# The first pass and the last stage of a Mamba-2, attention and expert decoder on one core: transposes inside a unit, five moved steps, contexts drawn ahead, ones columns beside the values

## The chip, the cores and the metric

The kernel is one program on one core of a Trainium2 chip. TensorE (PE in the rows) multiplies and transposes, VectorE (DVE) and ScalarE (ACT) read and write SBUF and PSUM, GpSimd (POOL) works on SBUF only, SyncE (SP) issues the DMAs. The metric is the device time of one execution in microseconds. Less is better.

## The reference, cut to what matters

Three residual layers run over 32 sequences of 64 tokens with 512 features, 2048 tokens in all. Most of the work is the first layer.

```python
x = x + mamba2(layernorm(x))              # 128 heads of 64, 8 groups, state 128
x = x + attention(layernorm(x), ctx)      # 32 query heads, 8 key heads of 16, per sequence
x = x + experts(layernorm(x))             # 4 low-rank experts (rank 16), top 2

proj = h @ in_proj_w.T                    # gate 8192, xBC 10240, dt 128
xBC = silu(conv4(xBC) + conv_b)           # depthwise, 4 taps
y = ssd(xs, A, B, C, D, softplus(dt))     # decayed scores per head, times x
g = y * silu(gate)
g = g * rsqrt(mean over each group's 1024 (g*g) + eps) * norm_w
return g @ out_w.T

scores = q k / 4 + mask;  probs = softmax(scores);  out = probs @ ctx
```

Keys and values of the attention are both the rows of `ctx` (64 by 128 for each sequence).

## The kernel before, in words

**The main loop.** Tokens are taken in four blocks of 512 (`tb`), and in each block the eight groups (`g`) follow one another: 32 iterations, `n = 8 tb + g`. An iteration has 18 *units* (`unit(k, ...)`), each 12 matmuls of 128x512 that project the block on 128 rows of `in_proj_w`. Unit 0 gives B, unit 1 C, and then even units give x for channel tile c, odd units the gate for it. Units alternate between the two PSUM banks `p_in[0]` and `p_in[1]`. An even unit's bank is read by ScalarE (`tap0`) and VectorE (`conv`), then `silu` makes `x_t`; `to_tokens(c)` transposes `x_t` on TensorE into `p_in[1]`; `x_tokens(c)` (VectorE) scales it into `x_tok`; `heads(c)` multiplies two channel tiles at a time with `decay` into `p_y`; `skipped` and `gated` (VectorE) make `t_y` and `g_f`. ScalarE and GpSimd split `g_f` in `g_hi` and `g_lo`, and `project(c)` multiplies both with `o_ring` into the four banks `p_out`, 12 matmuls, three for each 128 tokens.

`decay` is made in a chain for each block of 8 heads: GpSimd subtracts (`differences`), VectorE clamps (`clamped`), ScalarE takes the exponential (`exp`), VectorE multiplies by the scores (`decayed`). `exp` needs another function table than `silu`: each change is an ACT_TABLE_LOAD.

**The first pass** is the first iteration (n = 0, "not begun"). It has its own order, with `decay` of block 0 in two halves. All along it also splits the raw weights: ScalarE writes the high part, GpSimd (`w_low`, line 1722) and VectorE (`refill_o`, line 1258) the low part. `normal(QT, ...)` is the layernorm of the next block's first tile, which `normal_tile` transposes.

**The end.** Attention and experts of a tile of 128 tokens are spread over the main loop for 12 of the 16 tiles. The last four tiles (`q` = 0 to 3) can only start once the last group's output is summed. After the loop come: the last `heads`, `project(5)`, `experts_in` of loop tile 11, `project(6)`, `mean_squares` (the sum of squares over the group, as products of `ss` with a column of ones), `project(7)` tile by tile (`part_done`), and meanwhile the root mean square (`variance` on VectorE, `inverse_rms` on GpSimd). `accumulate_tile(q)` (VectorE, line 1667) is then the first step of each of the four tiles.

**The tables.** The four tiles' steps (k = 0 to 16) and the last three steps of loop tile 11 (17 to 19) are put in order by `waves`: for each engine a table of places, sorted. An engine does its steps in that order and in no other. The steps are: 0 accumulate, 1 context (transposed, copied, and made into `kbd` and `v2` by GpSimd), 2 query rows, 3 and 5 scores of each half, 4 and 6 maxima, shift and exponential, 7 and 8 transposed probabilities, 9 values, 10 and 11 divide and add, 12 expert rows, 13 low rank, 14 logits, 15 experts, 16 delta and result. Each tile has two PSUM banks `y0`, `y1`.

The softmax totals of these four tiles come out of TensorE: beside each 32 columns of values, a product of the same probabilities with two columns of `v2m` gives two totals.

The contexts of the four tiles are loaded by SyncE after the last `heads` (`load_context`: three DMAs for a tile, one of `ctx`, two of `v2r`), in the order q = 0, 1, 2, 3.

Of the kernel before, what the change touches and what calls it, by code (L numbers as in the profile page):

```python
# [38 lines left out]
def decoder_kernel(nc, x, ctxv, amask, wt, wdt, owt, params, dtb, alog, ffa, ffb,  # L39
# [10 lines left out]
    with outer:  # L50
# [72 lines left out]

        TILE_WIDE = (("sc", [2, 2, 2 * KV // 2, SEQ]), ("row", [HID]), ("col", [KT, P]), ("x2s", [HID]))
        TILE_REST = (("p_t", [REP, KV // 2, P]), ("ctx", [P]), ("ctx_t", [P]), ("v2r", [2, P]), ("v2", [2, P]), ("kbd", [2, KV // 2, SEQ]),
# [55 lines left out]
        v2_done = sem("v2_done"); kbd_done = sem("kbd_done"); part_done = sem("part_done"); sum_done = sem("sum_done")  # L181
# [50 lines left out]
        TAIL_PE = (56, (1452, 584, 672, 741, 1521, 826, 942, 895, 922, 959, 298, 1336, 1458, 1515, 1693, 1691, 1764, 1085, 0, 650))  # L232
        TAIL_ACT = (73, (851, 454, 558, 1395, 841, 215, 887, 854, 918, 2146, 1536, 514, 1382, 1475, 1572, 1741, 1676, 0, 106, 1977))
        TAIL_DVE = (97, (242, 0, 355, 575, 664, 746, 748, 691, 89, 2397, 972, 1001, 1094, 512, 1344, 1479, 1932, 347, 371, 492))
        TAIL_POOL = (105, (856, 981, 857, 1965, 1662, 1957, 1729, 2327, 670, 1771, 1993, 2018, 1301, 2835, 1361, 1816, 1018, 0, 232, 1822))

        def waves(stage, places):

            step, stages = places
            turns = [(at + step * q, q, k) for q in range(QT) for k, at in enumerate(stages) if q == 0 or k < 17]  # L240
            for _, q, k in sorted(turns):
                y0, y1 = ((p_in[0][:, :], p_in[1][:, :]), (p_y[:, 0, :], p_y[:, 1, :]),
                          (p_out[0][:, :], p_out[1][:, :]), (p_out[2][:, :], p_out[3][:, :]))[q]
                stage(k, q, LOOP_TILES + q, tail_tiles[q], y0, y1)
# [28 lines left out]
        def _(sp):  # L273
# [193 lines left out]
        def _(pe):  # L467
# [38 lines left out]
            def unit(k, tb, g, n):  # L506
# [24 lines left out]
                for w, a in ((0, 0), (0, 1), (1, 0)):  # L531
                    for kt in range(KT):
# [133 lines left out]
            def values(t, S, y0, totals=None):  # L666
# [3 lines left out]
                for r in range(REP):  # L670
                    for gp in range(KV // 2):
                        for s in range(2):
                            rows = slice(s * SEQ, (s + 1) * SEQ)
                            ins = mm(y0[rows, r * P + gp * 32:r * P + gp * 32 + 32], S.p_t[:, r, gp, rows],
                                     S.v2[:, s, gp * 32:(gp + 1) * 32], True, True)
                            if totals is not None:
# [508 lines left out]
        def _(dve):  # L1185
# [466 lines left out]
            for c in range(2):  # L1652
                dve.wait_ge(sq_done, CPG * ITERS - 1 + c)
                ins = V.tensor_tensor(ss[:, :], ss[:, :], g_sq[:, c, :], ALU.add)
                if c == 0:
                    link(ins)
# [279 lines left out]
```

## Time and profile before

| | us |
|---|---|
| median of 3 runs | 2863.83 |
| the 3 runs | 2863.83, 2866.99, 2861.97 |
| the profiled execution, its own time | 2870.87 |
| its span, first to last instruction | 2869.1 |

The profiled execution took 1.77 us more than its span, and is 7.0 us above the median of the runs. TensorE is busy 2828.2 us of the span (99%), VectorE 1999.2, ScalarE 1453.9, GpSimd 1316.5. From 200 to 2700 us TensorE has hardly a gap; the two stages that the change touches are the first 100 us and the last 85 us.

The profile's rows give for a group of instructions: start, length, engine, line, operation, tile written <- tiles read, shape, count, and in brackets the idle time just before with what ended it.

### The profile page before, as it was taken

The numbers are of one execution on the slowest core, as the hardware profiler recorded it, in microseconds if no ns is written. First come the engines' busy times: TensorE is split into PE (matmuls) and PEld (weight loads), VectorE is DVE, ScalarE is ACT, GpSimd is POOL, SyncE is SP. The second block draws the span as 40 slices with busy tenths as digits, with TensorE's granted clock in tenths as the row PEclk, the third lists the DMA queues.
The fourth block names the chain that finished last, engine by engine and source line by source line (L and its number), as shares of the span: only waits on it lengthen the run. The fifth ranks groups of instructions, "written<-read, shape, count | busy, mean of one in ns | idle before, by whom it ended". The sixth has DMA issues, their size and how long they took to land.

```text
span 2869.1 us, 56835 instructions
## 1 busy us (share of the span) xinstructions
PE 2828.2 (99%) x22480; PEld 2288.3 (80%) x22480; DVE 1999.2 (70%) x3154; ACT 1453.9 (51%) x2185; POOL 1316.5 (46%) x832
## 2 busy tenths in 40 slices
PE   7999999999999999999999999999999999999998
PEld 5788888778788788887888888888887888878876
DVE  7777768887667667677666666677666576666667
ACT  5666566655445535445445454544445354454443
POOL 4767767775344333443342443433444334433423
PEclk9999999999999999999999999999999999999997
DMA  7788777878566555555565564565665555555630
GB/s 242 266 303 290 264 269 258 274 254 289 182 196 194 177 184 184 184 184 187 194 198 185 187 198 162 187 194 171 200 199 181 185 188 186 185 190 170 197 105 20
DMA packets 179431, 578.30 MB, mean 202 GB/s; under 512 B 25249, under 2 KB 31905, under 8 KB 171105
## 3 DMA queue, kind: packets, MB, share of 16 engines
q1 hardware_dynamic: 179168, 574.66, 60.9%
q8 instruction: 182, 2.98, 0.4%
q14 instruction: 81, 0.66, 0.1%
HBM read 460.29 MB, written 114.29 MB: 200 GB/s over the span
## 4 chain that ended last, share of the span: by engine, by line
PE 92%; DVE 5%; ACT 1%; issue 1%; POOL 0%; DMA 0%; DVEq 0%; SPq 0%; ACTq 0%; POOLq 0%
PE p_in L469 53%; PE p_out L469 24%; PE p_y L469 9%; PE p_in L557 4%; DVE cv L1318 1%; PE p_y L663 1%; DVE o_ring L1258 1%; DVE t_y L1367 1%; DVE g_f L1379 1%; ACT cv L861 0%; DVE cum L1280 0%; DVE decay L1350 0%; PE p_y L685 0%; PE p_y L634 0%; DVE cum L1272 0%
## 5 line engine op out<-in xcount | busy, mean ns | idle before, releaser
L469 PE MATMUL p_in<-xnb,w_ring 128*128 128x512 f32 x6864 | 1683.4, 398 | 0.9 <-DVE cv L1318 0.9
L469 PEld LDWEIGHTS p_in<-xnb,w_ring 128*128 128x128 f32 x6864 | 1263.7, 189 | 266.5 <-issue 1.6
L1318 DVE SCALAR_TENSOR_TENSOR cv<-p_in,cpar,cv 128x504 f32<-128x504 f32 x954 | 700.0, 734 | 469.3 <-ACT cv L861 445.8
L1730 POOL TENSOR_TENSOR g_lo<-g_f,g_hi 128x512 fp32r<-128x512 f32 x256 | 342.5, 1339 | 1202.5 <-ACT g_hi L861 1202.5
L469 PE MATMUL p_out<-o_ring,g_hi 128*128 128x512 f32 x2048 | 639.0, 393 | 1.1 <-POOL g_lo L1730 1.1
L861 ACT ACTIVATE cv<-p_in,cpar 128x512 f32<-128x512 f32 x318 | 246.4, 775 | 642.0 <-PE p_in L469 604.4
L469 PEld LDWEIGHTS p_out<-o_ring,g_hi 128*128 128x128 f32 x2048 | 379.6, 188 | 81.8 <-issue 1.3
L469 PE MATMUL p_out<-o_ring,g_lo 128*128 128x512 f32 x1024 | 400.0, 391 | 0.0
L1355 DVE TENSOR_TENSOR x_tok<-p_in,dts 128x512 f32<-128x512 f32 x256 | 176.5, 690 | 290.0 <-PE p_in L557 288.5
L861 ACT ACTIVATE x_t<-cv 128x512 f32<-128x512 f32 x256 | 160.9, 628 | 309.3 <-DVE t_y L1367 285.9
L1741 POOL TENSOR_TENSOR ss<-ss,g_sq 128x512 f32<-128x512 f32 x190 | 309.3, 1628 | 7.5
L1784 POOL TENSOR_TENSOR decay<-decay,cumk 128x2048 f32<-128x2048 f32 x63 | 234.6, 3724 | 33.6 <-DMA decay<-cum_scr 33.6
L861 ACT ACT_TABLE_LOAD x183 | 234.8, 1283 | 4.0 <-PEq L1930 0.7
L1722 POOL TENSOR_TENSOR w_ring<-raw_w,w_ring 128x512 fp32r<-128x512 f32 x144 | 208.5, 1472 | 59.5 <-ACT w_ring L861 43.9
L861 ACT ACTIVATE sg<-p_in 128x512 f32<-128x512 f32 x254 | 149.0, 587 | 167.4 <-PE p_in L469 167.4
L469 PEld LDWEIGHTS p_out<-o_ring,g_lo 128*128 128x128 f32 x1024 | 192.2, 188 | 41.2
L1367 DVE SCALAR_TENSOR_TENSOR t_y<-x_t,dpar,p_y 128x256 f32<-128x256 f32 x512 | 210.9, 475 | 0.9 <-PE p_y L469 0.9
L1379 DVE TENSOR_TENSOR g_f<-t_y,sg 128x512 f32<-128x512 f32 x256 | 182.6, 754 | 0.0
L861 ACT ACTIVATE g_hi<-g_f 128x512 fp32r<-128x512 f32 x256 | 159.3, 623 | 34.4 <-DVE g_f L1379 33.9
L469 PEld LDWEIGHTS p_y<-decay,x_tok 64*64 64x64 f32 x8192 | 131.6, 135 | 49.3 <-issue 49.3
L557 PE MATMUL p_in<-id_sb,x_t 128*128 128x128 f32 x1024 | 158.0, 277 | 7.4 <-ACT sg L861 5.0
L557 PEld LDWEIGHTS p_in<-id_sb,x_t 128*128 128x128 f32 x1024 | 118.2, 141 | 50.7 <-issue 21.2
(259 smaller groups left out, 2298.9 us busy)
## 6 DMA issues: line engine op xcount, KB each, us to landing
w_ring<-ws_scr SPq DMA_DIRECT2D x432, 512.0 KB, 3.7
o_ring<-ows_scr SPq DMA_DIRECT2D x192, 512.0 KB, 4.6
ws_scr<-w_ring SPq DMA_DIRECT2D x144, 512.0 KB, 5.7
decay<-cum_scr SPq DMA_DIRECT2D x126, 512.0 KB, 6.8
raw_w<-wt SPq DMA_DIRECT2D x144, 256.0 KB, 5.0
ows_scr<-o_ring SPq DMA_DIRECT2D x64, 512.0 KB, 6.0
raw_o<-owt SPq DMA_DIRECT2D x64, 256.5 KB, 5.3
acb<-x SPq DMA_DIRECT2D x3, 1024.0 KB, 7.2
```

Source lines behind the costliest of these rows:

```text
L469: return nc.tensor.matmul(o, lhsT=l, rhs=r, start=first, stop=last)
L557: ins = nc.tensor.transpose(p_in[1][:, q * P:(q + 1) * P], x_t[:, c % 2, q * P:(q + 1) * P], id_sb[:, :])
L663: ins = nc.tensor.transpose(banks[rl][:, gp * P:(gp + 1) * P], pv, id_sb[:, :])
L861: return nc.scalar.activation(dst, src, func, **kw)
L1318: ins = V.scalar_tensor_tensor(acc[:, :, t:SEQ], src[:, :, 0:SEQ - t], cpar[:, 5 * m + 3 - t:5 * m + 4 - t], acc[:, :, t:SEQ], ALU.mult, A ...
L1355: V.tensor_tensor(x_tok[:, c % 2, :, :].rearrange("p q (h d) -> p q h d", h=2), p_in[1][:, :].rearrange("p (q h d) -> p q h d", q=QT, h=2) ...
L1367: ins = V.scalar_tensor_tensor(t_y[:, c % 2, :].rearrange(by_seq, q=QT, s=2)[:, s], x_t[:, c % 2, :].rearrange(by_seq, q=QT, s=2)[:, s], d ...
L1379: V.tensor_tensor(g_f[:, c % 2, :], t_y[:, c % 2, :], sg[:, (CPG * n + c) % GATES, :], ALU.mult).then_inc(g_done, 1)
L1722: T(w_ring[:, k % RING_W, 1, :, :].rearrange("p k c -> p (k c)"), raw_w[:, (UNITS * g + k) % RAW_W, :], w_ring[:, k % RING_W, 0, :, :].rea ...
L1730: T(g_lo[:, c % 2, :], g_f[:, c % 2, :], g_hi[:, c % 2, :].bitcast(F32), ALU.subtract).then_inc(glo_done, 1)
L1741: T(ss[:, :], a, g_sq[:, c % 2, :], ALU.add).then_inc(ss_done, 1)
L1784: T(decay[:, blk, :, :, :], decay[:, blk, :, :, :], last.unsqueeze(3).broadcast_to([P, 8, QT, SEQ]), ALU.subtract) \
```

## The change

What it does, by place:

- **First pass.** `to_tokens(1)` moves into unit 6, behind its first 4 matmuls (argument `between`). Unit 8 moves ahead of `to_tokens(2)`. `normal(QT, ...)` moves ahead of `conv(5)`. `clamped(1)` and the refill of `o_ring` 2 and 3 move from step 3 to step 4; `exp(1)` moves from step 3 to step 4 and `decayed(1)` from step 4 to step 5, and so does one load of the silu table.
- **Last iteration.** `to_tokens(7)` moves between the two halves of `project(4)`.
- **Behind the loop.** The contexts of q = 0, 1, 2 are transposed ahead of `project(6)`, all into `p_in[0]`, and copied by ScalarE in one stretch; the fourth becomes step 20 of the tables. VectorE's two additions of `g_sq` to `ss` are gone, and TensorE multiplies both `g_sq` halves with the ones as well (12 products of one column for 4), between the halves of `project(6)`. `skipped` and `gated`, `g_high` and `square` go channel by channel.
- **Ones columns.** `v2` gets 34 columns for each pair of heads, the last two filled by ScalarE (`ones_out`) with the columns of `v2m`, so one product of 34 columns replaces the two of 32 and 2. The reciprocal reads the two banks in two instructions.
- **Tables and banks.** New places for all four engines, written out for each tile, and tiles 1 to 3 in other banks. Step 17 is now the low rank part of loop tile 11.
- **SyncE** issues the same DMAs in the same order; the wait ahead of the fourth context is on `ms_done` in place of `ss_done`.

```diff
-        TAIL_PE = (56, (1452, 584, 672, 741, 1521, 826, 942, 895, ...
+        TAIL_PE = {2: (2, 4, 10, 13), 3: (3, 5, 12, 14), 5: (6, 9, 16, 20), ...
...
+        TAIL_BANKS = ((p_in[0][:, :], p_in[1][:, :]), (p_out[0][:, :], p_out[1][:, :]),
+                      (p_out[2][:, :], p_out[3][:, :]), (p_y[:, 0, :], p_y[:, 1, :]))
...
             for q in range(QT):
                 if q == 3:
-                    sp.wait_ge(ss_done, SUMS * ITERS)
+                    sp.wait_ge(ms_done, ITERS)
...
                 for w, a in ((0, 0), (0, 1), (1, 0)):
+                    if a == 1 and between is not None:
+                        to_tokens(between, n)
                     for kt in range(KT):
...
+            def values_totals(q, t, S, banks):
...
+                for r in range(REP):
+                    for gp in range(KV // 2):
+                        at = (r % 2 * (KV // 2) + gp) * VW
+                        for s in range(2):
+                            rows = slice(s * SEQ, (s + 1) * SEQ)
+                            ins = mm(banks[r // 2][rows, at:at + VW], S.p_t[:, r, gp, rows], S.v2[:, s, gp, :], True, True)
...
-                    unit(6, tb, g, n)
-                    to_tokens(1, n)
+                    unit(6, tb, g, n, 1)
...
+                    if k == 2 and not begun:
+                        unit(8, tb, g, n)
+                    if final(n) and k == CPG - 1:
+                        project(k - 3, tb, n, range(0, 2))
...
             experts_in(LOOP_TILES - 1, loop_tile, y0)
-
-            project(CPG - 2, NTB - 1, ITERS - 1)
-            mean_squares(ITERS - 1)
+            for q in range(QT - 1):
+                pe.wait_ge(tail_in[q], 48)
+                context_in(LOOP_TILES + q, tail_tiles[q], p_in[0][:, q * P:(q + 1) * P])
+
+            project(CPG - 2, NTB - 1, ITERS - 1, range(0, 2))
+            pe.wait_ge(ss_done, SUMS * ITERS - 2)
+            pe.wait_ge(sq_done, CPG * ITERS)
+            pe.sem_inc(hold, 1)
+            for h in range(QT):
+                tok = slice(h * P, (h + 1) * P)
+                mm(p_y[:, 1, h:h + 1], ss[:, tok], ones[:, :], True, False)
+                mm(p_y[:, 1, h:h + 1], g_sq[:, 0, tok], ones[:, :], False, False)
+                ins = mm(p_y[:, 1, h:h + 1], g_sq[:, 1, tok], ones[:, :], False, True)
+            ins.then_inc(ms_done, 1)
+            project(CPG - 2, NTB - 1, ITERS - 1, range(2, QT))
...
-                    if k == (2 if begun else 3):
+                    if k == (2 if begun else 4):
                         exp(1, n)
...
+            for c in (CPG - 2, CPG - 1):
+                g_high(c, ITERS - 1)
+                square(c, ITERS - 1)
+            act.wait_ge(ct_done, LOOP_TILES + QT - 1)
+            for q in range(QT - 1):
+                context_out(LOOP_TILES + q, tail_tiles[q], p_in[0][:, q * P:(q + 1) * P])
...
+                    if k == 3 and not begun:
+                        normal(QT, xt[:, :], xt[:, :], QT)
                     conv(2 + k, n)
...
-                    if k == (3 if begun else 4):
+                    if k == (3 if begun else 5):
                         decayed(1, n)
```

TensorE in the first pass, from the scores of B and C (`c_t,b_t`) to the first output product, before (`p_in<-id_sb,x_t` is a `to_tokens`, `p_y<-decay,x_tok` a `heads`):

```order
L469 MATMUL p_y<-c_t,b_t 64x64 x8
L557 MATMUL p_in<-id_sb,x_t 128x128 x4
L469 MATMUL p_in<-xnb,w_ring 128x512 x12
L557 MATMUL p_in<-id_sb,x_t 128x128 x4
L469 MATMUL p_y<-decay,x_tok 64x64 x32
L469 MATMUL p_in<-xnb,w_ring 128x512 x12
L557 MATMUL p_in<-id_sb,x_t 128x128 x4
L469 MATMUL p_in<-xnb,w_ring 128x512 x24
L469 MATMUL p_out<-o_ring,g_hi 128x512 x2
```

The same place of the changed kernel:

```order
L471 MATMUL p_y<-c_t,b_t 64x64 x8
L561 MATMUL p_in<-id_sb,x_t 128x128 x4
L471 MATMUL p_in<-xnb,w_ring 128x512 x4
L561 MATMUL p_in<-id_sb,x_t 128x128 x4
L471 MATMUL p_in<-xnb,w_ring 128x512 x8
L471 MATMUL p_y<-decay,x_tok 64x64 x32
L471 MATMUL p_in<-xnb,w_ring 128x512 x24
L561 MATMUL p_in<-id_sb,x_t 128x128 x4
L471 MATMUL p_in<-xnb,w_ring 128x512 x12
L471 MATMUL p_out<-o_ring,g_hi 128x512 x2
```

The second transposes stand 8 matmuls earlier, the third 12 matmuls later.

ScalarE in the first pass, from the splits of step 3 to the conv tap of step 5, before (`cv` is `tap0`, `sg` the gate, `decay` the exponential of block 1):

```order
L861 ACTIVATE w_ring<-raw_w 128x512 x4
L861 ACT_TABLE_LOAD
L861 ACTIVATE decay<-decay 128x2048
L861 ACTIVATE cv<-p_in,cpar 128x512
L861 ACT_TABLE_LOAD
L861 ACTIVATE spare<-half_neg 128x1
L861 ACTIVATE x_t<-cv 128x512
L861 ACTIVATE sg<-p_in 128x512
L861 ACTIVATE g_hi<-g_f 128x512
```

The same place of the changed kernel:

```order
L896 ACTIVATE w_ring<-raw_w 128x512 x4
L896 ACTIVATE cv<-p_in,cpar 128x512
L896 ACTIVATE x_t<-cv 128x512
L896 ACTIVATE sg<-p_in 128x512
L896 ACTIVATE g_hi<-g_f 128x512
```

The exponential and two table loads no longer stand ahead of the taps and the silu of step 4; they follow one step later.

TensorE behind the loop, before, from the rows of loop tile 11 (`row_l`) through `project(6)` to the products with ones and the first of `project(7)`:

```order
L685 MATMUL p_y<-id_sb,row_l 128x128 x4
L469 MATMUL p_out<-o_ring,g_hi 128x512 x2
L469 MATMUL p_out<-o_ring,g_lo 128x512
...
L469 MATMUL p_y<-ones,ss 128x1 x4
L469 MATMUL p_out<-o_ring,g_hi 128x512 x2
L469 MATMUL p_out<-o_ring,g_lo 128x512
```

The same place of the changed kernel (six matmuls of `project(6)` stand where the first gap is, six more behind the ones):

```order
L699 MATMUL p_y<-id_sb,row_l 128x128 x4
L632 MATMUL p_in<-id_sb,ctx 128x128 x3
L471 MATMUL p_out<-o_ring,g_hi 128x512 x2
L471 MATMUL p_out<-o_ring,g_lo 128x512
...
L471 MATMUL p_y<-ones,ss 128x1
L471 MATMUL p_y<-ones,g_sq 128x1 x2
```

Three transposes of contexts stand ahead of `project(6)`, each behind its tile's DMAs, and the products with ones have moved from behind `project(6)` into its middle and are three times as many.

## Rows read from the trace of the kernel before

**Rows 1.** Windows: stretch, length, busy PE, PEld, DVE, ACT, POOL, granted clock, DMA

```profile
200.00:2700.00 2500.00, 2495.57 (x19632) 2022.05 (x19634) 1733.22 (x2704) 1265.56 (x1888) 1131.55 (x703) 1.00 0.62 204
2795.59:2866.62 71.03, 62.24 (x802) 46.62 (x800) 56.60 (x144) 26.41 (x52) 26.98 (x24) 0.78 0.05 17
```

**Rows 2.** Timeline of PE, the first pass

```profile
49.92 0.60 PE L557 MATMUL p_in<-id_sb,x_t 128*128 128x128 f32 x4
52.52 1.65 PE L469 MATMUL p_y<-decay,x_tok 64*64 64x64 f32 x64 [2.01 <-DVE decay L1337]
...
82.28 0.63 PE L557 MATMUL p_in<-id_sb,x_t 128*128 128x128 f32 x4 [2.59 <-ACT sg L861]
82.66 7.35 PE L469 MATMUL p_in<-xnb,w_ring 128*128 128x512 f32 x24
...
102.94 5.76 PE L469 MATMUL p_in<-xnb,w_ring 128*128 128x512 f32 x24
```

**Rows 3.** Timelines of DVE, ACT and POOL, the first pass

```profile
50.55 0.69 DVE L1355 TENSOR_TENSOR x_tok<-p_in,dts 128x512 f32<-128x512 f32 x1 [3.15 <-PE p_in L557]
51.16 1.22 DVE L1337 TENSOR_TENSOR decay<-decay,cbt 128x1024 f32<-128x1024 f32 x1
...
56.03 4.29 DVE L1379 TENSOR_TENSOR g_f<-t_y,sg 128x512 f32<-128x512 f32 x2
...
74.98 1.92 ACT L861 ACTIVATE decay<-decay 128x2048 f32<-128x2048 f32 x1
...
55.48 3.70 POOL L1784 TENSOR_TENSOR decay<-decay,cumk 128x2048 f32<-128x2048 f32 x1
...
63.03 3.15 POOL L1730 TENSOR_TENSOR g_lo<-g_f,g_hi 128x512 fp32r<-128x512 f32 x2
```

**Rows 4.** SyncE's timeline behind the last heads; landing times of the v2r DMAs

```profile
2786.02 0.33 SPq L340 DMA_DIRECT2D ctx<-ctxv  x1
...
2790.56 1.25 SPq L342 DMA_DIRECT2D v2r<-ctxv  x2
...
DMA to landing us min/median/max: 2.2/2.3/3.4
```

**Rows 5.** Timeline of PE behind the loop

```profile
2784.81 1.16 PE L469 MATMUL p_y<-decay,x_tok 64*64 64x64 f32 x64 [0.83 <-issue]
...
2793.26 0.95 PE L469 MATMUL p_y<-ones,ss 128*128 128x1 f32 x8
...
2801.80 0.42 PE L698 MATMUL p_y<-id_sb,midg_l 128*64 128x128 f32 x1 [3.83 <-DVE midg_l L1543]
```

**Rows 6.** Windows of PE: length, busy, granted clock, DMA

```profile
2800.00:2801.00 1.00, 0.00 (x0) 0.85 0.00 0
...
2807.00:2808.00 1.00, 1.00 (x16) 0.74 0.04 10
...
2843.00:2869.00 26.00, 22.35 (x116) 0.50 0.11 41
```

**Rows 7.** Timelines of POOL and DVE in the last stage

```profile
2794.48 1.01 POOL L1745 TENSOR_TENSOR rms<-msv,half_neg 128x4 f32<-128x4 f32 x1 [2.93 <-DVE msv L1383]
...
2795.59 0.75 DVE L1667 SCALAR_TENSOR_TENSOR acb<-p_out,rms,acb 128x512 f32<-128x512 f32 x1 [1.18 <-POOL rms L1745]
...
2846.00 0.36 DVE L1684 RECIPROCAL rs<-p_out 128x32 f32<-128x32 f32 x1 [4.41 <-PE p_out L469]
```

**Rows 8.** The chain that ended last, with PE's timeline of the loop tile's values

```profile
2770.00 2.72 PE p_out L469 x12
...
2772.65 2.06 PE L469 MATMUL p_y<-v_l,p_t_l 128*64 128x32 f32 x64
...
2821.06 3.85 PE p_in L469 x128
```

**Rows 9.** PE's timeline, the product with wb at either clock

```profile
2741.07 1.12 PE L469 MATMUL p_y<-wb,m_t_l 64*128 64x512 f32 x2
...
2857.41 2.07 PE L469 MATMUL p_in<-wb,m_t 64*128 64x512 f32 x2
```

More of the change, by code:

```diff
@@ L504, in _, with unit @@
             step_sizes(0)
-            def unit(k, tb, g, n):
+            def unit(k, tb, g, n, between=None):
                 if tb == 0:
@@ L664, in probs, with values @@
                 ins.then_inc(pt_done[half], 1)
-            def values(t, S, y0, totals=None):
+            def values(t, S, y0):
                 pe.wait_ge(ptc_done[1], t + 1)
@@ L802, in body @@
                     to_tokens(k, n)
+                    if final(n) and k == CPG - 1:
+                        project(k - 3, tb, n, range(2, QT))
             iterations(pe, body)
@@ L840, in stage @@
                 if k == 9:
-                    values(t, S, y0, y1)
+                    values_totals(q, t, S, (y0, y1))
+                if k == 17:
+                    low_rank(LOOP_TILES - 1, loop_tile, p_y[:, 0, :])
                 if k == 18:
@@ L1035, in body @@
                     tap0(2 + k, n)
[L1036 to L1037 removed]
+                    if (k == 2 and (closing(tb, g) is not None or not begun)) or k == 3 or (k == 4 and tb >= 1 and is_at(tb, g, 4)) \
+                            or (k == 5 and (former(opening(tb, g)) is not None or not begun)):
                         silu_table()
@@ L1630, in body @@
                         spread(k, tb, g)
+                    if k == 4 and not begun:
+                        clamped(1, n)
+                        refill_o(3)
                     if k != 3:
@@ L1637, in body @@
                     late(k, tb, g)
-                    if k == 3 and not begun:
-                        clamped(1, n)
                     if k in (2, 3):
                         spread(k, tb, g)
-                    if k == 3:
+                    if k == 3 and begun:
                         refill_o(k)
@@ L1646, in _ @@
             expert_row(LOOP_TILES - 1, loop_tile)
-            skipped(CPG - 2, ITERS - 1)
-            skipped(CPG - 1, ITERS - 1)
-            gated(CPG - 2, ITERS - 1)
-            gated(CPG - 1, ITERS - 1)
-            dve.wait_ge(ss_done, SUMS * ITERS - 2)
[L1652 to L1656, printed above, removed]
-            ins.then_inc(ss_done, 2)
+            for c in (CPG - 2, CPG - 1):
+                skipped(c, ITERS - 1)
+                gated(c, ITERS - 1)
             variance(ITERS - 1)
```

107 lines of the change are left out of this document (60 added, 47 removed).

## The prediction

> **What bounds the kernel now.** I read the busy shares first, then windows by stage, then the timelines of both ends, then the waits. From 200 to 2700 us TensorE works 2495.57 of 2500 us [rows 1]: nothing that the change does to another engine can show there, and no matmul of the loop is removed. So the change can only win or lose in the first 100 us, where TensorE stops a few times, and from the last `heads` on (2784.81), where the bound changes hands. From the first accumulation of the last four tiles (2795.59) to the last result (2866.62) lie 71.0 us, in which VectorE works 56.60, TensorE 62.24 and at a mean granted clock of 0.78 [rows 1]. Neither is full: it is a chain over four engines, with VectorE carrying the most work that does not depend on the clock. A gain in the first pass stays a gain to the end, since the loop behind it is bound by TensorE alone.
>
> **First pass.** TensorE waits 2.01 us at 50.5 for `decay` and 2.59 us at 79.7 for the gate [rows 2].
>
> *Transposes inside unit 6.* VectorE sat idle 3.15 us until `x_tok` at 50.55, for the transposes that came only behind all 12 matmuls, and the product for `decay` (1.22) stood behind it [rows 3]. Now the transposes come 8 matmuls earlier, about 3 us. `x_tok` is then done before ScalarE's half exponential, the product runs at about 48.8 to 50.0, and `heads(0)` starts when unit 6 ends. Unit 6 ends later by its inner transposes (0.60 [rows 2]) and a short wait for the first `x_tok`: about 51.2. So `heads` at 51.2 for 52.5, a gain of 1.3, or 2.0 with the wait gone wholly.
>
> *Is it kept?* Behind it VectorE's two `g_f` products took 4.29 us, where others of that form take 1.3, because GpSimd had started its 3.70 us subtraction at 55.48, 0.5 us before them [rows 3]. They hold up `x_tok(2)`, and with it unit 9. VectorE now comes about 0.8 us earlier, GpSimd's two splits ahead of the subtraction about as before. I take it that at least one `g_f` is still caught: then unit 9 and `g_lo(0)` (63.03 [rows 3]), which opens `project(0)`, stand where they stood, and of the 1.3 us nothing is counted. The Trainium skill, *SBUF — State Buffer*, section "Who interferes with whom", says that the engine of the two that issues first holds the shared port pair for its whole instruction. By that rule VectorE, 0.8 us earlier, could be first for both; the price would be the gain of the rival "port" below.
>
> *Step 3 to step 4.* Here I expect most. ScalarE's exponential ended at 76.9 [rows 3], and behind it came the tap, VectorE's conv, the silu and the gate, for which TensorE waited until 82.28. TensorE's unit 10 had been done since 72.9. With the exponential and two table loads gone from there (ACT's 1.92 and two times 1.28), and the clamp and two splits gone from VectorE, the tap comes at 73.7, conv ends at 76.7, silu and gate at 78.8, while TensorE is busy until about 79.3 with `project(1)`. So the wait of 2.59 goes. The 24 matmuls behind it took 7.35 where undisturbed ones take 5.76 [rows 2]: the granted clock had fallen behind the wait, and 1.59 more comes back. Sum 4.2 at 90 us.
>
> *What is late next.* The clamp (2.3) now stands behind `x_tok(4)` and ends at 82.9; ScalarE waits for it, then 1.9 for the exponential, and only then can it take the tap of unit 12 (82.7): `x_t(5)` at 89.4, while TensorE is done with `project(2)` at 88.3. That gives back 1.2. Three splits of `o_ring` lie between, and `decayed(1)` stands ahead of `x_tok(5)`: its cover is unit 14 (2.8), and if that cover went it would cost up to 2.3. Net for the first pass: 4.2 - 1.2 = 3.0 us. Bounds: 0.5 (the wait at step 4 is only moved to step 5) and 5.5.
>
> **End, up to the first accumulation.** `to_tokens(7)` two thirds of a microsecond earlier fills the 0.83 us before the last `heads` [rows 5]: `heads` end at 2785.1 for 2785.9, everything behind it, SyncE too, 0.8 earlier.
>
> Then a new wait. SyncE issues the contexts after `heads`: first at 2786.02, the last `v2r` of tile 2 at 2791.2 (second of the pair at 2790.56), and it lands 2.2 to 2.3 us later, at 2793.5 [rows 4]. With 0.8 off it is 2792.7. TensorE reaches the transposes of the contexts after `project(5)` (2.72 [rows 8]) and `row_l`, at 2788.4. So it stands for 4.2 us, and behind it in its queue are `project(6)`, the ones, and `project(7)`, that is everything that VectorE's first accumulation needs. Before, `project(6)` began at 2790.45. From 2792.9: half of `project(6)` 1.37, the ones 2.4 (8 passes took 0.8 net of the next start, so 24 take 2.4 [rows 5]), half of `project(6)` 1.36, first tile of `project(7)` 0.68. The root mean square runs beside the last two (0.3 and 1.01 on GpSimd [rows 7]). First accumulation at 2798.8, against 2795.59: 3.2 later. VectorE's 2.1 us of additions and their 1.9 us wait, which the change removes, were on the old path and are inside this difference.
>
> The clock: TensorE's wait of 3.83 us that began at 2798.0 [rows 5] dropped the granted clock from full to half at about 2800.7 (0.85 in that window) and it returned at about 2807.5 (0.74) [rows 6]. A wait of 4.2 us that began at 2788.4 would drop it at about 2791.1 in the same way, and `project(6)` and the ones would run at half clock for 3 to 5 us. That costs 1.5 to 2.7. I take 2.0: first accumulation at 2800.8, 5.2 later than before. Bounds 2798.8 and 2801.5.
>
> The Trainium skill, *TensorE: Matmul & The Clock Gate*, section "HAM oscillation — how this bites in real kernels", warns of just this: each wait for a DMA between bursts of matmuls is paid a second time at half clock. By it the upper bound would hold in place of 2800.8.
>
> **End, from the first accumulation on: 73.5 us before (2795.59 to 2869.1).** What the four tiles have to do is the same on VectorE (reciprocals of 16 for one of 32 cost about nothing), 56.6 us with some 2.8 us in which it stood behind GpSimd. On TensorE a tile's values take 3.85, and 2.06 without the totals, as in the loop tile [rows 8]: 1.8 us times four, two to three of them on the old chain. Three contexts and two `kbd` are out of the way, where the old chain ran through ACT's copies and GpSimd from 2802.3 to 2811.6. I walked both orders by hand with the durations of the rows. VectorE then finds nearly all its inputs ready until the fourth tile's division (idle 4.41 before [rows 7]), and ends 56.5 us after the first accumulation at full clock. With the store behind it (2.5) that is 59.0. Then the additions: 1 us of standing behind GpSimd; 1 us for half clock in the early part, where TensorE stops between its steps, as ahead of the earlier drops; and the end. Before, the clock stayed at half from 2842 on (0.50 [rows 6]), and a product with `wb` took 2.07 for 1.12 [rows 9]. In my walk the last stretch of TensorE (four low ranks, four deltas, four rows) then ends 4.4 us later than at full clock, and it is what ends last. Nothing in the change keeps TensorE busier there, so I take 4.0. Sum 59 + 1 + 1 + 4 = 65.0 against 73.5, 8.5 less. Bounds: 60 (clock holds) and 69.5 (clock low early as well, and hand-overs of 0.1 us that I left out add up).
>
> The ones columns cost six small ScalarE copies ahead of the tables' start and GpSimd writes in pieces of 32; ScalarE works 26.4 of 71 us there [rows 1], so nothing is charged. In the main loop GpSimd's write of `v2` changes shape alone; TensorE's hundred-per-cent stretch hides it.
>
> **Sum.** End: +5.2 - 8.5 = -3.3. First pass -3.0. Together -6.3 in the profiled execution, 2870.9 to 2864.6. The profiled one lay 7.0 above the median of the runs; taken from the median, 2863.8 - 6.3 = 2857.5.
>
> **Rivals.**
>
> *Forecast (0.46):* as above, 2857.5; its own range is 2853.5 to 2861.
>
> *Port and clock go well (0.26).* VectorE's `g_f` products come ahead of the 3.70 us subtraction (a further 1 to 2 us), or the clock stays full in the new wait (2.0) or at the end (4.0). For it: the drop at the end hung on a gap of 1.2 us. Against it: TensorE has less to do there than before and stops more often. Two of the three give 5 more: 2852.
>
> *The gain is used up in the end (0.22).* The wait for the third context costs its 5.9, the last stage only gets 5 shorter because its hand-overs decide and not its work, and the first pass keeps 1.5: 2863.8 + 5.9 - 5 - 1.5 = 2863.2, between 2858 and 2864. For it: idle time of VectorE in this stage was 14.4 us (71.03 less 56.60), and a new order by hand rarely meets all of it.
>
> *Slower (0.06).* The clock falls in the new wait and TensorE, which stops often behind it, does not get it back. Its work behind the first accumulation, some 38.6 us at full clock, is 77 at half, and then it bounds the stage: 77 + 4 + 2.5 in place of 65.0, 18 later, less what a busy TensorE recovers. It decides from about 12 us more of half clock than forecast. Against it: at 2807 the clock came back under steady work. 2870.
>
> **Chances.** 0.2% is 5.7 us, about what a measurement of this kernel can tell from no change. Faster than 2858.1: six tenths of the forecast's 0.46, nearly all of the second case, almost none of the third: 0.27 + 0.25 + 0.02 = 0.54. Slower than 2869.6: most of the last case, 0.05. Same: 0.41. The range 2850 to 2864 leaves out 0.1 on either side.
>
> **What would show it.** TensorE's timeline should have no wait ahead of `heads(0)` and none over 1 us at 80; the clock should be full from 57 to 90. A wait of about 4 us on a context DMA should stand ahead of `project(6)`, the first `acb` at 5 us later counted from the last `heads`' old place, values at about 2.1 us a tile, VectorE idle under 8 us behind the first accumulation. The prediction is wrong if TensorE does not stand at the contexts, if the clock is full in the last 20 us, or if the wait at 80 only moves to 90.

## The result, and the profile after

The changed kernel takes 2878.81 us (median of 6 runs, 2877.35 to 2880.06) against 2864.76 (6 runs, 2861.97 to 2867.79) for the kernel before: ratio 1.0046, 95% interval 1.0035 to 1.0056. It is 14 us slower, where 6 us less were forecast. Its profiled execution took 2878.25 us, the span in it 2876.5.

The timeline of TensorE in the first pass, changed kernel (start, length, instruction, in brackets the idle time before it and what ended it):

```profile
49.48 1.16 PE L471 MATMUL p_y<-decay,x_tok 64*64 64x64 f32 x64
...
60.32 2.07 PE L471 MATMUL p_in<-xnb,w_ring 128*128 128x512 f32 x8 [3.13 <-DVE x_tok L1402]
...
99.86 1.12 PE L561 MATMUL p_in<-id_sb,x_t 128*128 128x128 f32 x4 [12.38 <-ACT x_t L896]
100.62 4.14 PE L471 MATMUL p_in<-xnb,w_ring 128*128 128x512 f32 x12
```

The wait for `decay` and the wait of 2.59 us at step 4 [rows 2] are gone; `project(2)` ends at 87.5 us. Counted from the scores (`p_y<-c_t,b_t`, at 42.00 us before and at 40.48 here) that is 47.0 us, where before it was 50.6. Then TensorE stands for 12.38 us ahead of `to_tokens(5)`, at the step behind the one that the change relieved, and the 12 matmuls behind the wait take 4.14 us, where before the same 12 took 3.00 (at 92.94).

Timelines of VectorE, SyncE and ScalarE in that place, changed kernel:

```profile
79.87 1.96 DVE L1391 TENSOR_SCALAR decay<-decay 128x2048 f32<-128x2048 f32 x1
81.75 3.49 DVE L1305 SCALAR_TENSOR_TENSOR o_ring<-raw_o,o_ring 128x512 fp32r<-128x512 f32 x2
...
85.27 0.33 SPq L291 DMA_DIRECT2D raw_o<-owt  x1
...
86.14 0.46 SPq L288 DMA_DIRECT2D raw_w<-wt  x1
...
91.70 0.63 ACT L896 ACTIVATE w_ring<-raw_w 128x512 fp32r<-128x512 f32 x1 [11.49 <-DMA raw_w<-wt]
92.24 0.71 ACT L896 ACTIVATE o_ring<-raw_o 128x512 fp32r<-128x512 f32 x1
92.96 1.28 ACT L896 ACT_TABLE_LOAD   x1
94.25 1.91 ACT L896 ACTIVATE decay<-decay 128x2048 f32<-128x2048 f32 x1
96.07 0.76 ACT L896 ACTIVATE cv<-p_in,cpar 128x512 f32<-128x512 f32 x1
...
99.17 0.63 ACT L896 ACTIVATE x_t<-cv 128x512 f32<-128x512 f32 x1 [0.34 <-DVE cv L1365]
```

Read it from the bottom. TensorE waits for `x_t` of unit 12. Its tap (96.07) stands in ScalarE's queue behind the moved exponential (94.25), and that behind the splits of the raw weights (91.70), for which ScalarE sat idle 11.49 us. Those weights were not slow (5.6 us from the issue to the split, and the median of these loads in the same stretch before is 5.6 too), they were asked for late: SyncE issued the load at 86.14, right behind two loads of `raw_o` that had to wait until VectorE had read the old `raw_o`. That reading is the refill of `o_ring` 2 and 3, which the change moves to step 4, behind the clamp: 81.75.

The end, changed kernel, timelines of TensorE and VectorE:

```profile
2792.67 1.16 PE L471 MATMUL p_y<-decay,x_tok 64*64 64x64 f32 x64
...
2797.61 0.33 PE L632 MATMUL p_in<-id_sb,ctx 128*128 128x128 f32 x1 [0.39 <-DMA v2r<-ctxv]
2799.41 0.34 PE L632 MATMUL p_in<-id_sb,ctx 128*128 128x128 f32 x1 [1.47 <-DMA v2r<-ctxv]
2801.47 0.47 PE L632 MATMUL p_in<-id_sb,ctx 128*128 128x128 f32 x1 [1.71 <-DMA v2r<-ctxv]
2801.59 1.20 PE L471 MATMUL p_out<-o_ring,g_hi 128*128 128x512 f32 x2
...
2804.30 0.42 PE L471 MATMUL p_y<-ones,ss 128*128 128x1 f32 x2
...
2809.28 1.20 PE L471 MATMUL p_out<-o_ring,g_hi 128*128 128x512 f32 x2
...
2813.56 0.75 DVE L1721 SCALAR_TENSOR_TENSOR acb<-p_out,rms,acb 128x512 f32<-128x512 f32 x1 [3.94 <-PE p_out L471]
```

Windows of the end, changed kernel (stretch, length, busy PE, PEld, DVE, ACT, POOL, granted clock, DMA):

```profile
2799.00:2800.00 1.00, 0.34 (x1) 0.14 (x1) 0.00 (x0) 0.25 (x1) 1.00 (x1) 0.80 0.37 105
2800.00:2812.00 12.00, 10.54 (x38) 9.38 (x39) 0.16 (x1) 1.69 (x10) 2.82 (x4) 0.50 0.08 22
...
2827.00:2862.00 35.00, 29.74 (x449) 22.92 (x449) 33.49 (x83) 20.77 (x36) 19.19 (x15) 1.00 0.03 10
```

The contexts are waited for, 3.6 us in three pieces; the clock falls to half (1.2 of 2.4 GHz) with them and stays there through all of `project(6)`, the 24 passes of ones (the 12 products of one column, each of which the trace shows as two passes: 4.98 us from 2804.30) and the start of `project(7)`. The first `acb` comes 20.9 us after the last `heads`; it was 10.8 [rows 5, 7]. From there to the end of the span it takes 62.9 us, where the profile of before has 73.5. The clock is not full in all of that: it is at half again from 2820.5 to 2826.5 and from 2864.3 on.

### The profile page after: what moved, and what is told of

It is laid out like the page before. It is cut to its first block, busy times and chain, and to the rows that moved or that the text cites. A ratio compares the mean times of both kernels' runs of the same rounds, so it can differ in the third digit from the quotient of the medians.

```text
span 2876.5 us, 56362 instructions
## 1 busy us (share of the span) xinstructions
PE 2819.9 (98%) x22240; PEld 2278.2 (79%) x22240; DVE 1995.8 (69%) x3156; ACT 1454.9 (51%) x2193; POOL 1315.9 (46%) x832
## 4 chain that ended last, share of the span: by engine, by line
PE 90%; DVE 6%; ACT 1%; issue 1%; DMA 0%; POOL 0%; SPq 0%; DVEq 0%; POOLq 0%; ACTq 0%
PE p_in L471 52%; PE p_out L471 23%; PE p_y L471 9%; PE p_in L561 4%; DVE cv L1365 1%; PE p_y L667 1%; DVE t_y L1414 0%; DVE g_f L1426 0%; DVE o_ring L1305 0%; DVE sc L1522 0%; ACT cv L896 0%; DVE mx L1530 0%; ACT L896 0%; DVE cum L1327 0%; DVE decay L1397 0%
```

## The experiments

Every ratio is to the kernel before on the same chip, in the same series of runs. There were four series, in which the median of before was 2864.76 (changed), 2865.93 (refill_back, exp_back, front_only, end_only), 2866.62 (sp_order, front_fixed, refill_ctx) and 2866.22 (rms_first, ones_sum); across series the ratios are to be compared, not the medians. The table also gives, for the one profile of each kernel, three distances that leave out how the execution began: from the scores to `to_tokens(5)`, from the last `heads` to the first `acb`, and from there to the end of the span.

| kernel | median us | ratio, 95% | scores to `to_tokens(5)` | `heads` to `acb` | `acb` to end |
|---|---|---|---|---|---|
| before | 2864.76 | 1 | 50.6 | 10.8 | 73.5 |
| before_again (1 run) | 2861.95 | | 49.9 | 10.8 | 68.5 |
| changed | 2878.81 | 1.0046 [1.0035, 1.0056] | 59.4 | 20.9 | 62.9 |
| refill_back | 2863.96 | 0.9991 [0.9983, 1.0000] | 44.9 | 20.6 | 65.1 |
| exp_back | 2878.47 | 1.0040 [1.0026, 1.0054] | 57.6 | 18.1 | 65.4 |
| sp_order | 2872.47 | 1.0018 [1.0009, 1.0028] | 52.5 | 20.6 | 65.3 |
| front_only | 2875.87 | 1.0036 [1.0024, 1.0049] | 58.8 | 10.8 | 70.0 |
| front_fixed | 2863.68 | 0.9995 [0.9986, 1.0004] | 47.8 | 10.8 | 73.4 |
| end_only | 2867.17 | 1.0004 [0.9996, 1.0013] | 51.0 | 20.0 | 62.9 |
| refill_ctx | 2860.73 | 0.9981 [0.9972, 0.9990] | 48.3 | 16.5 | 62.8 |
| rms_first | 2858.94 | 0.9973 [0.9962, 0.9983] | 47.6 | 13.1 | 63.7 |
| ones_sum | 2856.21 | 0.9966 [0.9953, 0.9978] | 47.7 | 10.5 | 65.6 |

**refill_back** puts one line back.

```diff
                     if k == 4 and not begun:
                         clamped(1, n)
-                        refill_o(3)
...
-                    if k == 3 and begun:
+                    if k == 3:
                         refill_o(k)
```

> The changed kernel with one edit: in the first iteration VectorE refills o_ring 2 and 3 at step 3 again, as before, instead of behind the clamp of step 4. Theory 1 (the refill is late, SyncE, which takes its work in order, waits for it before it issues the loads of step 3, and the raw conv weights then land late on ScalarE's split): the loads of step 3 are issued near 79 us instead of 86, the 12.4 us that TensorE waits before the seventh unit of the first pass (it ends at 99.86) goes down to under 4 us, the end of the loop comes 8 to 12 us earlier, and the time is 0.9957 to 0.997 of the changed kernel, 2867 to 2871 by its median. Rival 1 (the exponential of unit 12 on ScalarE, moved to step 4, is what holds up the tap and the tile behind it): VectorE's refill alone changes nothing, the wait stays at 10 us or more and the time within 2 us of the changed kernel. Rival 2 (the load of the raw weights is slow because of what else is moved at that time): the load takes 5.5 us wherever it starts, and the wait shrinks by the 7 us of its start at most, to 5 us.

Timelines of SyncE and TensorE with the refill at step 3:

```profile
71.07 0.47 SPq L288 DMA_DIRECT2D raw_w<-wt  x1
...
85.03 0.66 PE L561 MATMUL p_in<-id_sb,x_t 128*128 128x128 f32 x4 [0.80 <-ACT x_t L896]
```

The load that stood at 86.14 is issued at 71.07, TensorE waits 0.80 us where it waited 12.38, and the median is 14.9 us lower. One line carries the whole loss, and theory 1 holds. The load was issued earlier than I had expected (79), and the gain was larger than expected (8 to 12). Rival 1, as stated, is out. Rival 2 was right that a load takes some 5.5 us wherever it starts (the median is 5.6 here as well), but with the load issued 15 us earlier nobody waits for that: the start decides, not the length.

**exp_back** leaves the refill late and puts the exponential's group back.

```diff
-                    if k == (2 if begun else 4):
+                    if k == (2 if begun else 3):
                         exp(1, n)
...
-                        clamped(1, n)
                         refill_o(3)
...
+                    if k == 3 and not begun:
+                        clamped(1, n)
```

> The changed kernel with the other half of the moved group put back: the clamp, the exponential and the decayed gate of unit 12 stand at the steps of the kernel before (clamp at the end of step 3, exponential at step 3), and only the refill of o_ring 2 and 3 stays at step 4. Theory 1: the refill starts up to 2 us earlier, since no clamp stands ahead of it, but the loads of step 3 still wait for it; TensorE waits 10 us or more ahead of the seventh unit, and the time stays within 3 us of the changed kernel. Rival 1: the wait falls under 4 us and the time by 8 to 12 us.

```profile
86.90 0.46 SPq L288 DMA_DIRECT2D raw_w<-wt  x1
...
97.26 1.12 PE L561 MATMUL p_in<-id_sb,x_t 128*128 128x128 f32 x4 [8.12 <-ACT x_t L896]
```

(timelines of SyncE and TensorE). The refill does not start earlier: counted from the scores it starts 2.2 us later, since all of VectorE's step 4 comes later behind the exponential, and the load is issued 1.6 us later. The time is the same as the changed kernel's. But the wait is 8.1 us, not 10 or more. By the same count TensorE arrives 2.5 us later, and `x_t` comes 1.8 us earlier although its load was later. These 3.4 us are the exponential: with a table load ahead of it (1.91 and 1.28 us) it stood behind the late splits and ahead of the tap, and part of the 12.4 was its doing. With it back at step 3, TensorE waits 1.9 us for the gate at step 4 again (2.59 before). So rival 1 names a part of the wait, not what sets it.

**sp_order** asks whether it is SyncE's order that makes the late refill cost so much.

```diff
-                    outs_first = tb == 0 and (step == 3 or first(n) and step == 1)
+                    outs_first = tb == 0 and (step == 3 and not first(n) or first(n) and step == 1)
```

> The changed kernel with one edit on SyncE alone: at step 3 of the first iteration it issues the loads of the conv weights ahead of those of the output weights, so that the wait for VectorE's late refill of o_ring 2 and 3 (still at step 4) no longer stands ahead of them. Theory 1 (it is SyncE's order that turns the late refill into late conv weights): TensorE's wait of 12.4 us ahead of the seventh unit falls to under 4 us, and the time to within 4 us of the kernel with the refill put back (2864). Rival 3 (the late refill itself, or the later o_ring data, is what holds the pass up): the wait stays over 8 us or comes back as a wait for the output weights, and the time stays near 2878.

Timelines of SyncE, ScalarE and TensorE:

```profile
70.70 0.33 SPq L288 DMA_DIRECT2D raw_w<-wt  x1
...
82.10 0.33 SPq L291 DMA_DIRECT2D raw_o<-owt  x1
...
85.30 0.73 ACT L896 ACTIVATE o_ring<-raw_o 128x512 fp32r<-128x512 f32 x1 [6.02 <-DMA raw_o<-owt]
...
92.94 1.12 PE L561 MATMUL p_in<-id_sb,x_t 128*128 128x128 f32 x4 [6.94 <-ACT x_t L896]
```

The conv weights are asked for in time (70.70), and 5.4 us of the wait go; the median falls by 6.3 (8 by the ratios). Neither expectation came true as it stood. The other 6.94 us stay, since the late refill has a second way to TensorE: `raw_o` itself is loaded late (82.10), and ScalarE, which takes its work in order, stands 6.02 us at the split of `o_ring` with the exponential and the tap behind it. Theory 1 had half of the mechanism. The whole of it is two queues in order, SyncE's and ScalarE's, behind one buffer that was freed late. (The Trainium skill, *TensorE: Matmul & The Clock Gate*, section "Architectural detail: the array is 16× 32×32, not 1× 128×128", calls the queues of ScalarE and VectorE strictly first in, first out; for ScalarE the row of 85.30 agrees.)

**front_only, front_fixed, end_only** separate the two halves of the change. The first is the kernel before with the changed first pass; the second the same with the refill at step 3, as in the diff of refill_back; the third is the changed kernel with the first pass of before.

> The kernel before with only the changes of the first pass; the last iteration and the end are those of before. Theory 1 and its rivals alike: the loop ends 8 to 9 us later than before, as in the changed kernel (8.7 us there), and the time is 8 to 14 us above the kernel before, ratio 1.003 to 1.005. If the end's changes are what costs, this kernel lies within 3 us of before.

> The kernel before with the changed first pass, but with the refill of o_ring 2 and 3 left at step 3; the last iteration and the end are those of before. With the refill put back, the loop of the changed kernel reached the transposes of row_l at 2779.6 us; here they should start near 2780.4, since the last iteration's move is out (0.84 us). The end of before took 80.3 us from there in the profile of before and 76.9 us in the one with the changed first pass. Theory (the end's changes cost more than they give): 2859 to 2863 us, 0.997 to 0.999 of before, and 2 to 5 us under the kernel with the refill put back and the changed end. Rival (the end's changes are a gain): 2865 us or more.

> The changed kernel with the whole first pass of before; it keeps the transposes of unit 7 moved in the last iteration, the contexts drawn ahead, the ones columns and the new orders of the end. If the end is as the trace of the changed kernel shows it (heads of the last unit to the end of the span 83.8 us against 84.3, and the heads 0.84 us earlier): 1 to 2 us below the kernel before, ratio 0.9993 to 0.9997. If the rest of the loss, 14 us in the medians against 7.4 in the profiles, sits in the end: 3 to 7 us above it.

The first pass as changed costs what the whole change costs, as expected (1.0036 of 1.0046; the intervals overlap). Without the moved refill it takes 47.8 us from the scores to `to_tokens(5)`, against 50.6 and 49.9: 2 to 3 us gained, which the ratio of front_fixed, 0.9995, does not resolve. With the end of before (front_fixed) or the changed end (refill_back, 0.9991) the time is the same, so neither the expected 2 to 5 us nor its rival came. The changed end alone is even (1.0004, interval from 1 us under to 4 us over): a loss of more than 4 us is excluded, a gain of 1 is not told from none.

**before_again** is the kernel before, unchanged.

> The kernel before once more, for one profile. The first profile of it lay 6 us above its median; it had TensorE at half clock through 12 of the projections at 14.7 us (4.91 us against 3.03), a gated product of VectorE that took 4.17 us beside a wide operation of GpSimd, and half clock in the last 26 us. If these three are accidents of one execution, the new profile differs in at least one of them by 1.5 us or more, and its span differs by what they are worth. If they belong to the kernel, all three come again and the span is within 2 us of 2869.1.

First the first profile of before (timeline of TensorE, then a window), then the new one:

```profile
14.71 4.91 PE L469 MATMUL p_y<-xnb,wd 128*128 128x512 f32 x12 [0.78 <-ACT xnb L861]
...
2842.00:2851.00 9.00, 9.00 (x99) 8.75 (x98) 4.25 (x13) 1.86 (x4) 0.76 (x2) 0.50 0.01 2
```

```profile
14.12 3.04 PE L469 MATMUL p_y<-xnb,wd 128*128 128x512 f32 x12 [0.78 <-ACT xnb L861]
...
2842.00:2851.00 9.00, 5.62 (x38) 4.09 (x36) 7.64 (x44) 3.02 (x13) 0.55 (x1) 0.97 0.01 2
```

The span is 2860.1 us, 9.0 less than the first: 4.0 by the last `heads` (2780.81 against 2784.81), of which 1.9 in these 12 matmuls, and 5.0 behind them. The program did not change. Behind the `heads` the granted clock did: in the first profile its first fall, at 2800.7, lasted 6.8 us and it stayed at half from 2842 on [rows 6], here the first fall lasted 3.4 us and the last came only just before 2851. Where the half clock of the end begins thus goes with the execution and not with the program; the profile of front_fixed, with the same end, has it early as well (from 2839, and 73.4 us). Of the 12 matmuls at the start only the durations differ: the column of the granted clock reads 1.00 for them in both profiles, so that the half clock that I had put them down to isn't shown. The third suspect, `g_f` beside GpSimd's wide subtraction (4.18 us), came again, so that one belongs to the kernel.

**refill_ctx** has the refill back, and the contexts behind `project(6)`.

```diff
-            for q in range(QT - 1):
-                pe.wait_ge(tail_in[q], 48)
-                context_in(LOOP_TILES + q, tail_tiles[q], p_in[0][:, q * P:(q + 1) * P])
             project(CPG - 2, NTB - 1, ITERS - 1, range(0, 2))
...
             project(CPG - 2, NTB - 1, ITERS - 1, range(2, QT))
+            for q in range(QT - 1):
+                pe.wait_ge(tail_in[q], 48)
+                context_in(LOOP_TILES + q, tail_tiles[q], p_in[0][:, q * P:(q + 1) * P])
```

> The changed kernel with the refill put back to step 3, and the three context transposes moved from ahead of the seventh output projection (project(6)) to behind it, ahead of project(7). Theory (the waits for the contexts, 3.2 us, and the half clock behind them, 12.4 us of TensorE's work from 2784.3 that would take about 6.2, cost the end its gain): no wait there, full clock through project(6), the first acb 6 to 9 us earlier after the heads, and the time 4 to 8 us under the kernel with the refill put back: 2856 to 2860 us. Rival (the chain of the loop's last tile and the tail tiles sets the end, not TensorE's arrival at the first acb): the first acb comes earlier, but the span falls by less than 2 us. Second rival (the loads land as late as before for project(7)): the waits reappear there, 1 us or more in all, and half of the gain is lost.

Timelines of TensorE, GpSimd and VectorE:

```profile
2787.67 0.58 PE L471 MATMUL p_y<-ones,g_sq 128*128 128x1 f32 x4
2788.12 0.36 PE L471 MATMUL p_y<-ones,ss 128*128 128x1 f32 x2
2788.34 0.97 PE L471 MATMUL p_y<-ones,g_sq 128*128 128x1 f32 x4
2789.18 1.20 PE L471 MATMUL p_out<-o_ring,g_hi 128*128 128x512 f32 x2
...
2793.18 1.04 POOL L1805 TENSOR_TENSOR kbd<-ctx_t,bd 128x512 f32<-128x512 f32 x1 [6.33 <-ACT ctx_t L895]
2794.18 0.73 POOL L1807 TENSOR_TENSOR v<-v2r,v2m 128x256 f32<-128x256 f32 x1
2794.86 1.01 POOL L1793 TENSOR_TENSOR rms<-msv,half_neg 128x4 f32<-128x4 f32 x1
...
2795.97 0.75 DVE L1719 SCALAR_TENSOR_TENSOR acb<-p_out,rms,acb 128x512 f32<-128x512 f32 x1 [6.46 <-POOL rms L1793]
```

No wait for a context is left. The first `acb` comes 4.1 us earlier after the `heads` (6 to 9 expected), the median 3.2 us lower than refill_back's (4 to 8 expected). The ratios, 0.9981 and 0.9991, put it at 3 us, with intervals that still overlap. Two things kept the rest. The clock still fell, now within the passes of ones (0.97 for four of them, 0.58 ahead), with no wait but 0.45 us in the 5 us before. And GpSimd stood at `kbd` for the contexts with `rms` behind it, whose input had been there since 2789.5.

**rms_first** moves `rms` ahead of `kbd`, on top of refill_ctx.

```diff
-        TAIL_POOL = {..., 17: (1,)}
+        TAIL_POOL = {..., 17: (-1,)}
```

> The kernel with the refill put back and the contexts behind the seventh output projection, and one more edit: GpSimd computes the inverse rms ahead of the first context's products (kbd and v), not behind them. In the profile without this edit msv was there at 2789.5 us, GpSimd stood at kbd for the contexts until 2793.2, took 1.04 and 0.73 us for them, and rms came at 2794.86, so the first acb started at 2795.97, 2 us after the first p_out of project(7) was there. If GpSimd's order is what holds the first acb: it starts 1.5 to 2.2 us earlier after the heads (16.5 us there) and the time falls by 1 to 2 us, to 2858.5 to 2860. Rival: the loop tile's own chain sets the end, the acb comes earlier and the time stays within 0.5 us.

```profile
2793.57 0.75 DVE L1719 SCALAR_TENSOR_TENSOR acb<-p_out,rms,acb 128x512 f32<-128x512 f32 x1 [3.39 <-PE p_out L471]
```

(timeline of VectorE). `acb` no longer waits for `rms` but for the matmuls. The distance shrinks by 3.5 us (1.5 to 2.2 expected), of which some came from a clock that fell about 2 us later, though nothing differs on TensorE ahead of it. The time is 2858.94, inside the expected 2858.5 to 2860, but the step from refill_ctx (0.9981 to 0.9973) is within the intervals.

**ones_sum** goes back to the sum on VectorE and 8 passes, on top of rms_first.

```diff
-                mm(p_y[:, 1, h:h + 1], ss[:, tok], ones[:, :], True, False)
-                mm(p_y[:, 1, h:h + 1], g_sq[:, 0, tok], ones[:, :], False, False)
-                ins = mm(p_y[:, 1, h:h + 1], g_sq[:, 1, tok], ones[:, :], False, True)
...
             project(CPG - 2, NTB - 1, ITERS - 1, range(2, QT))
+            mean_squares(ITERS - 1)
...
+                ins = V.tensor_tensor(ss[:, :], ss[:, :], g_sq[:, c, :], ALU.add)
```

> The same kernel as the one with the inverse rms first, but with the mean squares done as in the kernel before: VectorE adds the two squares to ss (2.1 us), and TensorE sums with 8 passes behind the whole of project(6), in place of 24 passes in its middle (3.1 us at full clock). Theory (the one-column passes themselves bring TensorE's clock down: at full clock the first 14 took 1.9 us, and half clock began with the last four at 2788.3 us, with no wait ahead of them but 0.45 us): no half clock ahead of project(7)'s end, the first acb 1 to 3 us earlier after the heads, the time 1 to 3 us less. Rival (the 24 passes are the gain that they seem, since VectorE's sum is gone from the chain): the clock falls anyway or VectorE's sum is waited for, the first acb comes later by up to 1 us, and the time is the same or 1 us more.

Timelines of TensorE and VectorE, and a window:

```profile
2788.59 1.02 PE L471 MATMUL p_y<-ones,ss 128*128 128x1 f32 x8
...
2791.00 0.75 DVE L1718 SCALAR_TENSOR_TENSOR acb<-p_out,rms,acb 128x512 f32<-128x512 f32 x1 [1.19 <-POOL rms L1792]
...
2784.00:2795.00 11.00, 9.32 (x51) 7.21 (x49) 7.65 (x14) 3.32 (x13) 6.08 (x7) 1.00 0.23 64
```

The clock is full up to 2801, and the first `acb` stands 10.5 us behind the `heads`, even a little nearer than before. That is 2.6 us nearer than in rms_first, so up to there the 24 passes cost more than VectorE's sum that they saved. Behind it 1.9 us are lost again (65.6 against 63.7), and of the median's 2.7 us not all is certain: the runs of the two kernels overlap (2855.45 to 2858.46 and 2855.90 to 2860.26). Taken together, the steps from refill_back to here are clear of noise. This is the fastest version: 2856.21 us, 0.9966 [0.9953, 0.9978].

## Why the prediction was wrong

*The step that failed* is "Three splits of `o_ring` lie between", in *what is late next*. I put the refill of `o_ring` 2 and 3 among the things that happen to lie in VectorE's queue and charged nothing. But it also frees `raw_o`; SyncE waits for that with the conv weights queued behind, and ScalarE waits for both loads with the exponential and the tap queued behind. The forecast gave 1.2 us back at `to_tokens(5)`; the kernel gave 12.38 us, and 1.1 more in matmuls at half clock. My bounds (0.5 to 5.5 us gained) asked only by how much the removed wait might come back. With the 10.1 us lost up to the first `acb` and the last stage's gain, the distances add up to the result: against before_again 9.5 + 10.1 - 5.6 = 14.0 us. The result lies beyond all four cases, and the "slower" case had another mechanism that did not occur.

*The rest of the first pass was right.* The wait at step 4 is gone and the 24 matmuls behind it take 5.76 us. The early transposes brought `heads(0)` forward by 1.5 us, from 10.5 to 9.0 behind the scores, and it was lost at `x_tok` (3.13), so counting nothing was right. With the refill left at step 3, TensorE waits 0.8 to 1.4 us for `x_t` of unit 12, against my 1.2, and in four profiles the pass is 1.6 to 3.4 us shorter (47.6 to 48.3 against 49.9, 50.6 and end_only's 51.0), against my 3.0.

*The port rival* (VectorE's `g_f` ahead of GpSimd's wide subtraction) occurred once. In the profile of refill_back VectorE's two `g_f` took 1.94 us, and GpSimd's subtraction (3.80) started at 54.11 while the second was at its end; in the changed kernel GpSimd started at 54.89, between the two, and the second took 4.17. Timelines of VectorE and GpSimd, changed kernel:

```profile
54.11 5.46 DVE L1426 TENSOR_TENSOR g_f<-t_y,sg 128x512 f32<-128x512 f32 x2
...
54.89 4.14 POOL L1835 TENSOR_TENSOR decay<-decay,cumk 128x2048 f32<-128x2048 f32 x1
```

refill_back's first pass was 2.7 to 3.4 us shorter than the other ones with the refill put back: TensorE waited 0.88 us for `x_tok` in place of 3.13, and its clock was back at full 5.2 us behind the scores, not 8.0 as in the changed kernel, with VectorE at `g_f` 1.4 us earlier. An early clock alone is not enough: in sp_order it was back as early, and GpSimd still came between the two. The Trainium skill, *SBUF — State Buffer*, "Who interferes with whom", says that the engine that issues first holds the shared ports and the other waits; both traces agree. I had priced this at 1 to 2 us; the wait alone shows 2.25.

*The new wait of the end* was sized well, 3.6 us for 4.2. *The clock behind it* was mis-sized: I let it come back after 3 to 5 us and took 2.0. It stayed at half until about 2813. From 2801.59, where `project(6)` starts, to the first `acb` at 2813.56 there were 12.0 us, filled by `project(6)`, the ones and the first tile of `project(7)`; I had 5.8 for the same work at full clock. That is 6.2 in place of 2.0, and with 0.6 less wait it makes nearly all of the difference between my 16.8 us from `heads` to `acb` and the 20.9 measured. The Trainium skill, *TensorE: Matmul & The Clock Gate*, "HAM oscillation — how this bites in real kernels", has a wait for a DMA paid again at half clock, and I had read that as my upper bound, 2801.5. The trace agrees with the rule and goes beyond that bound. How long the half clock lasts is no constant of this end either: with the same wait ahead it was 13.7 us in the changed kernel, refill_back and sp_order, 10.2 in end_only, and 3.4 in exp_back, whose first `acb` came after 18.1 us. But the wait was not the only cause: refill_ctx has no such wait and its clock fell too, in the passes of ones. In exp_back's profile the clock came back at 2802.0, the passes of ones ran at full clock up to 2804.51, and it fell again at 2805.4 though TensorE had not stood since 2799.03 and no context was transposed there. Windows of PE in exp_back (length, busy, granted clock, DMA):

```profile
2802.00:2805.40 3.40, 3.40 (x29) 1.00 0.02 5
2805.40:2808.70 3.30, 3.30 (x10) 0.50 0.20 60
```

With 8 passes (ones_sum and the end of before) it held past the first `acb` in all five profiles. I had charged the ones 2.4 us of TensorE and nothing for the clock.

*The last stage* was right in itself: 62.9 us against my 65.0, values of 2.06 us a tile, and VectorE idle for 6.0 us up to its last result, where it had been 14.4. The half clock at its end covered only the last 12 us. What the stage is to be compared with was wrong. I took before's 73.5 from one execution. The same end takes 68.5, 70.0 and 73.4 in other profiles: the two long ones have the last half clock from 2842 and 2839 on, the two short ones from 2851 and 2863 on. The changed end takes 62.8 to 65.6 us over all its profiles, so the gain of this stage is between 3 and 11 us by which profiles are compared, and with the 10 us lost ahead of it the end as a whole is even, as end_only shows (1.0004). My forecast was -3.3.

The expectation in the last lines of the prediction, that it would be wrong "if the wait at 80 only moves to 90", named the place; I gave it no chance of its own beyond a gain of 0.5.

What stays open: why 12 matmuls near the start take 3.0 us in some executions and 4.6 to 5.3 in others (2 us in effect), and whether it is the number of the one-column passes or their place in the middle of `project(6)` that goes with the fall of the clock. ones_sum changed both. The context transposes alone are not what brings it down: ones_sum has the same three right behind its 8 passes, and exp_back's second fall came without them.

## What to carry to other kernels

When an instruction is moved, ask what its *reading* frees, not only who reads its result: here a copy whose result nobody needed for long was what let two loads start. Follow each buffer that it frees through the queue of the engine that refills it, and then through the queue of the engine that uses the refill, and charge everything that stands behind. And compare a stage with several executions of the kernel before, when the clock in it can fall at more than one place: up to 5 us of the gain that I forecast were half clock that one profile had and another did not.

## What the hardware showed that I had not expected

- The same 12 matmuls at 14 to 15 us, with the same 0.78 us of idle time ahead, took 3.03 to 3.04 us in seven profiles and 4.64 to 5.29 in the five others, across kernels that do not differ there.
- Passes of ones with one column: where 24 in a row began at full clock, the granted clock fell to half in the last four of them (refill_ctx, 3.1 us in all), 1.3 us behind them (rms_first, 2.7 us) and 0.9 us behind them (exp_back, 2.65 us), with no wait over 0.45 us in the 5 us ahead in the first two. With 8 (0.95 to 1.02 us) it did not, in five profiles. What the cause is in the passes, no run here shows.
- Once at half, the clock did not come back for 11 us of TensorE's uninterrupted work in the changed kernel (9.00 busy of 9 us from 2804 to 2813, the passes of ones among it); in exp_back it came back after 3 us of work behind the same wait.
